# Two convolution chunks moved into a triangular inversion, and one projection moved ahead of eight transposes

## The reference, cut to what matters

```python
mixed = jnp.einsum('bsh,ch->bsc', x, W_qkv)
z = jnp.einsum('bsh,vh->bsv', x, W_z)
conv = sum((xp[:, k:k + Ss, :] * conv_w[:, k] for k in range(KCONV)))
mixed = jax.nn.silu(conv)
q, k, v = jnp.split(mixed, [KEY_DIM, 2 * KEY_DIM], axis=-1)
...
A = -(jnp.einsum('bhnid,bhnjd->bhnij', k_beta, kc) * decay) * strict
Tm = jax.scipy.linalg.solve_triangular(eye - A, eye, lower=True, unit_diagonal=True)
u = jnp.einsum('bhnij,bhnjv->bhniv', Tm, v_beta)
...
normed = core * jax.lax.rsqrt(var + EPS) * norm_w * jax.nn.silu(zr)
return jnp.einsum('bsv,hv->bsh', normed, W_out)
```

## Time and profile before

| what | value |
| --- | --- |
| median of 3 runs | 2388.04 us (2384.26 to 2389.48) |
| the profiled execution's own time | 2385.96 us |
| its span in the trace | 2383.9 us |
| PE busy | 2033.3 us (85%) |
| DVE busy | 1458.6 us (61%) |
| ACT busy | 879.0 us (37%) |
| mean granted TensorE clock | 0.896 of full |

### The profile page before, as it was taken

The page is one execution under the profiler, slowest core; times in us unless marked ns, Lnnn a source line. Parts: engine busy times, 40 slices in busy tenths (PEclk is TensorE's granted clock), DMA queues, the critical chain, the costliest instruction groups (busy, mean ns, idle before and its releaser), DMA issues. The chain is left out here.

```text
span 2383.9 us, 28590 instructions
## 1 busy us (share of the span) xinstructions
PE 2033.3 (85%) x10850; PEld 1513.1 (63%) x10850; DVE 1458.6 (61%) x3251; ACT 879.0 (37%) x1540; POOL 140.0 (6%) x130
## 2 busy tenths in 40 slices
PE   6988988898994979899898998989989884787786
PEld 4867777554552658586685866858668672455464
DVE  3567665223222576867768677676776854767666
ACT  2433433111112535354454534545345431332233
POOL 1011010100002000000000000000000001011010
PEclk8889888899996889999999999999999996777787
DMA  3000000400001120201203012030121202000000
GB/s 128 6 14 10 6 5 5 187 0 9 0 1 66 36 54 14 67 28 36 54 14 79 16 36 54 16 83 10 36 54 27 54 1 69 7 12 14 7 5 5
DMA packets 163259, 78.81 MB, mean 33 GB/s; under 512 B 140530, under 2 KB 152628, under 8 KB 162132
## 3 DMA queue, kind: packets, MB, share of 16 engines
q1 hardware_dynamic: 163124, 76.99, 11.8%
HBM read 59.88 MB, written 16.91 MB: 32 GB/s over the span
## 5 line engine op out<-in xcount | busy, mean ns | idle before, releaser
L1566 DVE TENSOR_TENSOR c_Y<-c_V,c_bank 128x512 f32<-128x512 f32 x192 | 131.8, 686 | 82.3 <-PE c_bank L1239 82.3
L1239 PE MATMUL c_bank<-c_Y,c_NP 128*128 128x128 f32 x1536 | 176.4, 276 | 0.0
L1239 PEld LDWEIGHTS c_bank<-c_Y,c_NP 128*128 128x128 f32 x1536 | 173.9, 192 | 3.4 <-issue 3.4
L1540 DVE SCALAR_TENSOR_TENSOR c_NP<-c_NP,c_cj,c_bank 128x256 f32<-128x256 f32 x256 | 104.8, 475 | 67.0 <-ACT c_NP L1410 67.0
L1172 PE MATMUL c_bank<-c_xT,c_wqk 128*128 128x512 f32 x256 | 127.2, 644 | 5.1 <-ACT c_pad L1366 3.1
L1501 DVE SCALAR_TENSOR_TENSOR c_cv<-c_pad,c_wcqk,c_cv 128x1024 f32<-128x1024 f32 x96 | 122.2, 1280 | 12.0 <-ACT c_cv L1380 11.2
L1501 DVE SCALAR_TENSOR_TENSOR c_cv<-c_pad,c_wcv,c_cv 128x1024 f32<-128x1024 f32 x96 | 122.5, 1283 | 2.6
L1326 PE MATMUL c_bank<-c_wout,c_yT 128*128 128x256 f32 x512 | 121.3, 383 | 0.0
L1172 PE MATMUL c_bank<-c_xT,c_wv 128*128 128x512 f32 x256 | 112.0, 595 | 4.1 <-DVE c_acc L1594 3.6
L1232 PE MATMUL c_bank<-c_wz,c_xT 128*128 128x512 f32 x256 | 111.2, 592 | 0.0
L855 ACT ACTIVATE b_sg<-b_G 128x512 f32<-128x512 f32 x50 | 29.7, 597 | 220.6 <-PE b_G L808 220.5
(11 more groups left out here) (409 smaller groups left out, 4226.6 us busy)
## 6 DMA issues: line engine op xcount, KB each, us to landing
b_wup<-b_in_wup SPq DMA_DIRECT2D x4, 1280.0 KB, 13.5
c_wqk<-c_in_wqk SPq DMA_DIRECT2D x9, 512.0 KB, 3.4
c_wv<-c_in_wv SPq DMA_DIRECT2D x8, 512.0 KB, 3.5
c_wz<-c_in_wz SPq DMA_DIRECT2D x8, 512.0 KB, 4.1
c_wout<-c_in_wout SPq DMA_DIRECT2D x8, 512.0 KB, 3.7
diagonal_blocks<-c_NP SPq DMA_DIRECT2D x64, 64.0 KB
c_A<-diagonal_blocks SPq DMA_DIRECT2D x8, 512.0 KB, 3.4
c_NP<-no_blocks SPq DMA_DIRECT2D x32, 128.0 KB, 3.8
```

What stands on the lines that cost most here:

```text
L1239: last = pe.matmul(banks[n % 4][:, b * P:(b + 1) * P], lhsT(h, 4 * q + b), rhs(h, 4 * q + b), start=True, stop=True)
L1540: dve.scalar_tensor_tensor(NP[:, h, bb, :, :], spread(NP[:, h, bb, 1, :], 2), cj[:, h, bb:bb + 1], gp, ALU.mult, ALU.mult).then_inc(s["NP_ ...
L1566: dve.tensor_tensor(rr(Y, h, q), rr(V, h, q), four(banks[n % 4][:, :]), ALU.subtract).then_inc(s["y_ready"], 1)
```

## The change

DVE does the convolutions of value chunks 0 and 1 inside the inversion, ahead of its step j = 10 (`BL // 3`), and no longer behind L1554. PE does the next round's first projection between the transposes of value chunk 0 and those of chunk 1, no longer behind both. Nothing is added or left out.

```diff
                 values(i, 0)
-                values(i, 1)
                 if more:
                     project(i + 1, 0)
+                values(i, 1)
                 pe.wait_ge(s["Tb_placed"], at(i, 16 * NBL, 16 * NBL))
...
                 for j in range(BL - 1):
+                    if j == BL // 3:
+                        conv(i, QK)
+                        conv(i, QK + 1)
                     n, w = BL - 1 - j, j + 1
...
                 elim.close()
-                conv(i, QK)
-                conv(i, QK + 1)
                 for n in range(HB):
```

## The result

The changed kernel takes 2391.49 us against 2387.23 for the kernel before (medians of 20 runs each), +4.3 us: a ratio of 1.0016, 95% interval 1.0008 to 1.0023. The forecast on the median was +3.5 us and 2391.5.

The account below looks back on a forecast made before the run. Limits differ by stage (PE busy 85%, DVE 61%); ACT sets the pace from the placed product on. Rounds 2 to 7 give 0, round 1 +0.6, round 8 +3.1: +3.7, rounded to +3.5 on 2388.0, 2391.5 us; range 2387 to 2395.

Parts of the forecast that it names:

- zero for rounds 2 to 7: Net per round: placed product 1.3 us sooner, low clock costs 1.3 us; 0, bounds -1.3 and +1.0.
- term for round 8: No next projection there; `c_Tb` lands late, so the SiLU of chunk 2 comes 3.1 us later, bounds +1.9 and +4.2.
- Taps inside the solve cost DVE nothing: Six taps (7.76 us) move into the solve without waiting; DVE reaches `c_V` of chunk 0 as before.
- The projection runs in idle time: PE's next projection takes 3.60 us at full clock in formerly idle time, delaying the transposes of chunk 1 by nothing.
- `c_Tb` lands 7.35 us after the store, product at 39.3 us: Store of `c_T` moves 7.76 us later; the placed product waits for the `c_Tb` loads, yet starts 1.3 us sooner.
- The clock in front of the product: PE idles 3.9 us before the placed product, so its first two quads run partly at low clock: +1.3 us.
- Settling of the round length: The low stretch slips until round length and stretches fall in step, damping gains and losses in rounds 2 to 7.
- sign of being wrong: Clock staying at 1.00 over the product, product waiting for something other than `c_Tb` loads, or round length settling elsewhere.
- Round 1: Product starts 0.2 to 1.1 us sooner, low clock takes 1.9 to 2.0: about +1.2 us, about half given back later.
- Rivals: Gain stays: 2381, chance 0.22; low clock covers whole product: 2399, 0.28; taps wait inside the solve: 2399, 0.04.
- second rival: Low clock covers the whole placed product, +2.3 instead of +1.3, or `c_Tb` lands 1 us later: +11.3 us, chance 0.28.

Follow-up runs that it names:

- filled wait: Changed kernel plus four 512-column matmuls on PE between the transposes of chunk 1 and the wait for `c_Tb`: 2383.00 us, ratio 0.9972 to the kernel before.
- putting round 8 back: Changed kernel, but in round 8 alone the taps of both chunks stand behind the solve as before: 2388.46 us, ratio 1.0003 to the kernel before.
- second stretch filled: Kernel before plus two 512-column matmuls ahead of PE's wait for `C_ready` in every round but the last: 2386.14 us, ratio 0.9998.

## Why the prediction was right, point by point

- **Total.** +3.5 forecast, +4.3 measured, with an interval of +1.9 to +5.5, and inside the 0.2% that got the largest chance (0.45). The number is partly luck: the zero for rounds 2 to 7 is the sum of two effects of 4 us and more, of which the prediction had one and sized it at nothing (see the settling below). The term for round 8 is no luck.
- **Taps inside the solve cost DVE nothing.** Right: `c_V` at 32.97 us against 32.98, no wait at the taps. With the DVE part alone, rounds 2 to 7 kept their length.
- **The projection runs in idle time.** Right: 3.60 us at the full clock, transposes of chunk 1 in 1.08 to 1.09 us in rounds 2 to 7.
- **`c_Tb` lands 7.35 us after the store, product at 39.3 us.** Nearly: from store to product 7.22 to 8.44 us, mean 7.80 over 8 rounds, product at 39.05 to 40.28 in rounds 2 to 7.
- **The clock in front of the product, +1.3 for -1.3.** Mechanism right, size low. In rounds 2 to 7 the wait was 4.1 to 5.3 us rather than 3.9, and the 24 records took 4.36 to 5.49 us. From product to SiLU 2 passed 4.00 to 4.31 us instead of 2.48, so the low clock cost 1.75 us in the mean and not 1.3, and the product gained 1.0 and not 1.3. SiLU 2 came 0.74 us later in the mean, where zero was forecast and +1.0 was the bound. The filled wait shows that it is the clock.
- **Settling of the round length.** Partly wrong, and this is the step that failed: "round length again near 146.8 for rounds 3 to 7". The mean of rounds 2 to 7 is 146.70, but they go from 146.19 to 147.59 and never settle, which the prediction had named as a sign of being wrong. It let one low stretch slip and took the other as constant. In the changed kernel the second one comes in rounds 3, 4 and 7 and not in 1, 2, 5 and 6; that returned 4.2 us in rounds 2 to 7, about what SiLU 2 had lost (4.5). Why it stays away in just these rounds, and so whether the balance is more than chance, is not shown. Rounds do settle in two kernels whose product doesn't wait for a DMA: with the projection alone (143.25 to 143.28) and with the second stretch filled (146.76 to 146.78). In the changed kernel the store goes at 31.83 to 31.85 us of every round from 2 on, and the product follows when `c_Tb` lands, 7.22 to 8.44 us later. That this varying time keeps the rounds from settling is a reading of the rows; no run tests it.
- **Round 1, +1.2.** At SiLU 2 it was +0.84; the round still ended 0.79 us sooner, because its rest was 1.63 us shorter, without the second stretch.
- **Round 8, +3.1.** Measured +3.60 at SiLU 2, and putting round 8 back takes 3.7 us off the total. By the medians this one term carries the result.
- **Rivals.** None came true. The second rival's price at SiLU 2 (+1.0 a round) was met in 3 of 6 rounds, 2, 5 and 6, but paid back in the rest. It was met there by the way that the rival names last, a late `c_Tb` (8.18 to 8.44 us after the store); the low clock never cost more than 1.83 us, inside the +1.9 allowed for two quads. What no case saw is how much the two parts work against each other: the projection alone gives -31.9, the taps alone +3.5, together +4.3. The prediction had both numbers for it (PE ready at 1153.4, `c_Tb` at 1149.5 before the taps moved) and used them only to size a wait.

## What to carry to other kernels

Before a slow step is delayed for work that "has to be done anyway", look at what hangs on its end: here 7.8 us of DVE work ahead of the end of a solve delayed a store, a reload and the first matmuls behind it, and took back some 36 us that the other half of the same edit had won. Spend slack only up to the point where the waiting engine arrives: half of the move (3.9 us) kept nearly all of it hidden. And when an edit makes TensorE wait in one piece ahead of a burst (here 4 to 5 us), price the burst at the low clock too, or give it work to do in the wait.

## What the runs showed of the hardware that was not expected

The rounds of this program can run into one length that goes with where the low clock falls: 146.75, 146.75, 146.76 in the kernel before, 143.25 to 143.28 in one variant, 146.76 to 146.78 in another whose rest was 0.92 us shorter. There the saving didn't show in the time, because 10.2 us of the round ran at the low level all the same. Where edits took both stretches away, rounds took 140.4 us.

The second low stretch follows a wait of 0.73 us and 1.92 us of one-column matmuls in PE's records; in the kernel before the granted clock is 0.50 behind them. With two matmuls of 512 columns in that wait (1.88 us in the records) it stays at 1.00. The edit fills the idle time and adds work at once, so it doesn't say which of the two counted. Two sets of one-column matmuls in a row ahead of a product of 128 columns cost 3.2 us a round (143.66 against 140.42).
